# Second tower's attention: score tiles per key head, value products on 128 rows, sums from a product with ones

## The chip, the cores and the metric

The kernel runs on one core of a Trainium2 chip. The metric is device time in microseconds (us) of one execution, the median of several. The engines of the core work side by side and meet only through semaphores: TensorE (PE: matmuls, and PEld: the loads of their weights), VectorE (DVE), ScalarE (ACT), GpSimd (POOL) and SyncE (SP, which here issues most of the DMAs). A matmul reads its weights and its moving columns from SBUF and writes to PSUM, which has eight banks of 512 fp32 columns by 128 partitions.

## What is computed

A small vision tower of two levels over 16 images of 96x96, each 37 tokens (36 patches and a class token) of width 256, so 592 tokens in all. The first level is patch embedding, an attention with ternary weights and a mixture of eight experts. The second level, to which the change belongs, is two attention layers and a last linear layer:

```python
# per layer: H = 16 heads of width 16, KV = 4 key heads, 4 query heads share one
q, k = rope(q), rope(k)
q, k = qk_norm(q), qk_norm(k)           # divide by the root of the mean square
scores = einsum('bhqd,bhkd->bhqk', q, repeat(k)) / 4
scores = where(causal (and within 64 for the second layer), scores, -1e30)
probs = softmax(scores)
x = x + merge_heads(einsum('bhqk,bhkd->bhqd', probs, repeat(v))) @ wo
```

With 37 tokens the window of 64 in the second layer cuts nothing off, so both layers run the same attention; they differ in how keys and values are projected (layer 1 through a latent of width 64).

## The kernel before

The whole program is one block with one instruction stream for each engine, written out by hand; the order of the work on an engine is the order of its code, and all waits are explicit semaphore waits. The second tower is the function `l1(li)`, which each engine has for itself and calls for li = 0 and 1.

**Ahead of the attention.** Queries and keys are rotated, squared, averaged (a matmul with `mean16`) and normalised in ten units of 296 columns: `project`, `mean_square` on TensorE, `square` and `inverse_root` on ScalarE (an Ln from PSUM, L625, and an Exp, L628), `rotate` and `normalise` on VectorE (L1167, L1173). The result `qk` has 128 partitions, 32 for each key head, and five planes: plane u is the u-th query head of each of the four key heads, plane 4 the keys. `fold_keys` brings the keys into `km`, a zero-filled tile with, for each image and each pair g of key heads, 64 columns for each of the two heads e; each head's keys stand in its own 32 partitions only, by copies on ScalarE (L633) and VectorE (L1186). `take_values` (L1179) copies the values into `vo`: partitions 0 to 36 hold the even key head of a pair, 64 to 100 the odd one, with 16 columns of values and 16 columns of ones for each (the ones are written once by POOL at the start of the program). In VectorE's order `take_values` comes after the eleventh step of the unit loop (u == U + 1), two normalisations still around it.

**The attention** goes over four groups of four images. For TensorE a group is `scores(grp)` and then, one group behind, `values(grp - 1)`.

- Scores: for each image two calls, one for each pair of key heads. Weights are `km[:, b, g]`, 128 rows by 128 columns, moving columns the four query planes of the image, 148. The zeros in `km` keep the heads apart. One PSUM bank (0 to 3) holds one image: 296 columns, keys of the two heads of a pair in the two halves of the partitions.
- ScalarE takes the exponential of a bank (L668, 128x296) into `ex`, VectorE multiplies by the causal mask (L1204).
- Values: for each image two calls, weights `vo[:, b, g]`, 128 rows by 64 columns, moving 148 columns of `ex`. Of the 32 output rows of a key head 16 are values and 16 the sum of the exponentials, 16 times over, because the weights are ones. The results go to banks 4 to 7, a group taking two of them.
- ScalarE evicts them into `oz` (L652, two calls a group), VectorE moves the sums onto the value rows with a stream shuffle within 32 partitions (L1211, 128x592), ScalarE takes Ln and Exp(-x) of them for the inverse (L658, L660, 128x592), and VectorE multiplies `oz` by it into `ozp` (L1216, 128x592). ScalarE and VectorE run this over six steps: exponentials of group grp, eviction of grp - 1, inverse of grp - 2.

**After it** the output projection: for each of the five token tiles four calls (L1838) over the four planes of `ozp`, 128 weights by 256 columns; half of the contracted rows are the sums' rows, for which `wo` holds zeros. A tile waits only for the divisions of the groups that it covers. VectorE adds each tile to the residual (L755) and takes its statistics (L737); both stand behind the last division in its queue. TensorE meanwhile runs filler matmuls (`keep_clock`, L1331), and then the next stage's transposes start.

SP loads the weights of the second tower (`wq`, `wo` and others, L412) after the last expert's weights, at about 250 us, while POOL's indirect DMAs gather the expert rows (L1307) for which VectorE then waits (L1038).

Of the kernel before, what the change touches and what calls it, by code (L numbers as in the profile page):

```python
# [11 lines left out]
ALU = mybir.AluOpType  # L12
# [4 lines left out]
B = 16  # L17
# [86 lines left out]
def tower(nc, xT, tokW, sel, posb, const, iota, pairrows, small, wq0, u2t, wo0, rw, wexp,  # L104
          wqg, kvd, kug, vug, wog, wql, wvl, wol, wfin, out):
    ctx = ExitStack()
    with ctx:
# [39 lines left out]
        vo = sb("vo", [P, B, KV // 2, 2, R])  # L147
# [116 lines left out]
        ozp = ab("ozp", [P, KV, TP])  # L264
        ab("gap_a", [P, 2 * WX - 2 * U5 * T - KV * TP])
# [16 lines left out]
        l1w = DC * P * (2 * KV + 1) + 2 * KV * D + DC * LAT + P + 2 * KV * DH + DC * KV * DH - KV * DH + TP + TT * D + 2 * DC * D  # L282
        ab("gap_b", [P, 2 * WX - l1w])
        arena_b = ab("stage_l1b", [P, 2 * KV * 2 * 4 * N + 8 * T])
# [5 lines left out]
        oz = arena_b[:, 2 * KV * QT:2 * KV * QT + 4 * T].rearrange("p (u t) -> p u t", u=4)  # L290
        zs = arena_b[:, 2 * KV * QT + 4 * T:2 * KV * QT + 8 * T].rearrange("p (u t) -> p u t", u=4)
# [141 lines left out]
        def _(act):  # L433
# [176 lines left out]
            def l1(li):  # L610
# [34 lines left out]
                def evac_o(grp):  # L645
                    for i in range(2):
                        act.wait_ge(S("o_mm"), 8 * li + 2 * grp + i + 1)
                        src = bank(4 + 2 * (grp % 2) + i)[:, 0:QT].rearrange(
                            "p (a u n) -> p a u n", a=2, u=4)
                        b = 4 * grp + 2 * i  # L650
                        dst = oz.rearrange("p u (b n) -> p b u n", b=B)[:, b:b + 2]
# [10 lines left out]
                for grp in range(6):  # L662
                    if grp < 4:
                        for g in range(KV):
                            act.wait_ge(S("s_mm"), 16 * li + 4 * grp + g + 1)
                            if grp >= 2:
                                act.wait_ge(S("o_mm"), 8 * li + 2 * (grp - 1))
                            A(ex[grp % 2][:, g, :], bank(g)[:, 0:QT], ACT.Exp,  # L668
                              scale=0.25).then_inc(S("ex"), 1)
                    if 1 <= grp <= 4:  # L670
                        evac_o(grp - 1)
                    if grp >= 2:
                        inverse(grp - 2)
# [7 lines left out]
        def _(dve):  # L681
# [454 lines left out]
            def l1(li):  # L1136
# [38 lines left out]
                def take_values():  # L1175
                    dve.wait_ge(S("v1_mm"), li + 1)
                    for e in range(2):
                        r = slice(KS * e, KS * e + N)
                        last = V.tensor_copy(vo[r, :, :, e, 0:DH].rearrange("p b g d -> p (b g) d"),  # L1179
# [8 lines left out]
                for u in range(U + 3):  # L1188
# [7 lines left out]
                    if u == U + 1:  # L1196
# [10 lines left out]
                def sums(grp):  # L1207

                    dve.wait_ge(S("o"), 8 * li + 2 * grp + 2)
                    s = (slice(None), slice(None), slice(grp * 4 * N, (grp + 1) * 4 * N))  # L1210
                    V.stream_shuffle(zs[s], oz[s], [DH + i % DH for i in range(32)]).then_inc(S("zs"), 1)  # L1211

                def divide(grp):
                    s = (slice(None), slice(None), slice(grp * 4 * N, (grp + 1) * 4 * N))
                    dve.wait_ge(S("zi"), 4 * li + grp + 1)
# [794 lines left out]
```

## Time and profile before

| | us |
|---|---|
| median of three runs | 385.9 |
| all three | 385.74, 387.66, 385.9 |
| the profiled execution | 390.73 |
| span of its instructions | 388.9 |
| TensorE busy | 355.0 (91%) |
| VectorE busy | 234.6 (60%) |
| ScalarE busy | 182.3 (47%) |
| POOL busy | 132.0 (34%) |
| mean granted clock of TensorE | 0.939 |

Busy shares are averages over stages with different limits; TensorE's also counts filler matmuls. The second tower begins at about 277 us: layer 1 lasts to about 323 us, layer 2 to about 372, the last linear layer to the end. Each fp32 matmul of the program shows in the trace as two records with a weight load each. The granted clock is 1.00 at 2.4 GHz and 0.50 at 1.2 GHz.

### The profile page before, as it was taken

How to read it: one execution, taken by the hardware profiler on the slowest of the kernel's cores; microseconds unless marked ns; L12 is line 12 of the kernel's file. 1: busy time of each engine (PE TensorE's matmuls, PEld its weight loads, DVE VectorE, ACT ScalarE, POOL GpSimd, SP SyncE). 2: the span in 40 equal slices, each digit the busy share in tenths (PEclk: the TensorE clock that was granted, in tenths of full speed). 3: DMA queues.
4: the chain of work that ended last, by engine and by line, in shares of the span. 5: the costliest groups of instructions: out<-in, count | busy, mean ns of one | idle time of the engine just before them, and what ended most of it. 6: DMA issues, size and time to landing. Idle time of an engine off the chain costs nothing.

```text
span 388.9 us, 7444 instructions
## 1 busy us (share of the span) xinstructions
PE 355.0 (91%) x3038; PEld 298.5 (77%) x3038; DVE 234.6 (60%) x587; ACT 182.3 (47%) x381; POOL 132.0 (34%) x67
## 2 busy tenths in 40 slices
PE   4898989998799797999999999959899998999996
PEld 3673668876499797999899999956467985789854
DVE  1278793796666742556645555456546876548844
ACT  2010772357233143666676676311178841768500
POOL 0601029202506703787577778544200001000010
PEclk9999995798769988999999999987999999999988
DMA  8980004200222412476566571480000000000001
GB/s 282 405 300 0 3 2 148 87 3 3 81 67 73 118 71 81 121 244 200 183 202 202 186 248 43 118 312 3 1 2 2 0 3 0 0 4 0 2 0 62
DMA packets 16012, 37.55 MB, mean 97 GB/s; under 512 B 1930, under 2 KB 9729, under 8 KB 15976
## 3 DMA queue, kind: packets, MB, share of 16 engines
q1 hardware_dynamic: 14432, 33.93, 25.8%
q0 software_dynamic: 960, 2.43, 1.9%
q10 hardware_dynamic: 584, 0.69, 0.6%
q8 instruction: 25, 0.41, 0.4%
q14 instruction: 11, 0.09, 0.1%
HBM read 31.29 MB, written 5.75 MB: 95 GB/s over the span
## 4 chain that ended last, share of the span: by engine, by line
PE 55%; issue 14%; DVE 14%; ACT 8%; DMA 5%; POOL 2%; SPq 1%; POOLq 0%; ACTq 0%; DVEq 0%
PE ps L1536 9%; PE ps L1537 8%; PE ps L1538 8%; PE ps L1437 2%; PE ps L1838 2%; PE ps L1736 2%; DMA stage_l<-in_tokW 2%; PE ps L1338 2%; PE ps L1331 2%; DMA yrowhi<-yg_d,of_hi 2%; PE ps L1462 2%; PE ps L1805 2%; PE ps L1858 2%; DVE ps L1049 2%; PE ps L1449 2%
## 5 line engine op out<-in xcount | busy, mean ns | idle before, releaser
L1259 POOL TENSOR_TENSOR w1l<-raw,w1h 128x1536 fp32r<-128x1536 f32 (+1 forms) x12 | 39.8, 3318 | 35.5 <-ACT w1h L533 33.6
L1049 DVE TENSOR_TENSOR ps<-gact,ps 128x256 f32<-128x256 f32 (+3 forms) x60 | 26.3, 438 | 40.3 <-ACT gact L557 39.4
L1259 POOL TENSOR_TENSOR w0l<-raw,w0h 128x1536 fp32r<-128x1536 f32 (+1 forms) x12 | 39.9, 3322 | 29.4 <-ACT w0h L533 29.4
L1269 POOL TENSOR_TENSOR rstd<-vtmp,cst 128x5 f32<-128x5 f32 x4 | 4.7, 1172 | 112.9 <-DVE vtmp L768 64.4
L557 ACT ACTIVATE gact<-ps 128x256 f32<-128x256 f32 (+3 forms) x60 | 23.3, 388 | 25.4 <-PE ps L1538 24.8
L561 ACT ACTIVATE hrh<-ps 128x256 fp32r<-128x256 f32 (+1 forms) x48 | 18.4, 384 | 33.8 <-DVE ps L1049 33.8
L1054 DVE TENSOR_TENSOR hrl<-ps,hrh 128x256 fp32r<-128x256 f32 (+1 forms) x48 | 20.3, 423 | 18.5 <-ACT hrh L561 18.5
L1331 PE MATMUL ps<-cst 128*128 128x512 f32 x66 | 30.3, 605 | 0.0
L1536 PE MATMUL ps<-xg0h,w1h 128*128 128x256 f32 x88 | 26.4, 301 | 0.0
L1536 PE MATMUL ps<-xg1h,w0h 128*128 128x256 f32 x88 | 25.6, 291 | 0.0
L1537 PE MATMUL ps<-xg0l,w1h 128*128 128x256 f32 x88 | 25.6, 291 | 0.0
L1538 PE MATMUL ps<-xg0h,w1l 128*128 128x256 f32 x88 | 25.5, 290 | 0.0
L1537 PE MATMUL ps<-xg1l,w0h 128*128 128x256 f32 x88 | 24.9, 283 | 0.0
L1538 PE MATMUL ps<-xg1h,w0l 128*128 128x256 f32 x88 | 24.9, 283 | 0.0
L1338 PE MATMUL ps<-stage_l 128*128 128x256 f32 x60 | 17.5, 455 | 6.7 <-DMA stage_l<-in_tokW 6.7
L1331 PEld LDWEIGHTS ps<-cst 128*128 128x128 f32 x66 | 12.1, 190 | 13.0 <-issue 12.8
L1338 PEld LDWEIGHTS ps<-stage_l 128*128 128x128 f32 x60 | 13.6, 232 | 9.8 <-issue 5.1
L1805 PE MATMUL ps<-stage_l1a,km 128*128 128x148 f32 x128 | 18.0, 292 | 0.7 <-DVE vo L1179 0.7
L1805 PEld LDWEIGHTS ps<-stage_l1a,km 128*128 128x128 f32 x128 | 16.6, 188 | 2.2 <-DVE vo L1179 1.2
L1536 PE MATMUL ps<-w0h,hrh 128*128 128x256 f32 (+1 forms) x48 | 14.4, 300 | 4.1 <-DVE hrl L1054 4.1
L1536 PE MATMUL ps<-xTh,w0h 128*128 128x296 f32 x44 | 14.9, 339 | 3.4 <-DVE hsl L1054 3.4
L533 ACT ACTIVATE w0h<-raw 128x768 fp32r<-128x768 f32 (+1 forms) x24 | 18.0, 801 | 0.0
(295 smaller groups left out, 1003.1 us busy)
## 6 DMA issues: line engine op xcount, KB each, us to landing
raw<-in_wexp SPq DMA_DIRECT2D x18, 768.0 KB, 4.2
raw<-in_wexp SPq DMA_DIRECT2D x9, 640.0 KB, 4.3
xg_d<-zero SPq DMA_DIRECT2D x8, 256.0 KB, 7.7
xgs<-xg_d SPq DMA_DIRECT2D x8, 256.0 KB, 4.5
stage_l<-in_xT SPq DMA_DIRECT2D x6, 320.0 KB, 6.0
yg_d<-y SPq DMA_DIRECT2D x7, 256.0 KB, 3.3
stage_l<-in_tokW SPq DMA_DIRECT2D x6, 128.0 KB, 7.7
wq_l<-in_wql SPq DMA_DIRECT2D x1, 640.0 KB, 6.2
```

Of the source, the lines that this page charges most:

```text
L533: A(wset[x % 2][0][:, o:o + n], raw[:, o:o + n], ACT.Copy).then_inc(S("w_hi"), 1)
L557: A(gact[i % 2][rows_of(c), 0:n], gate[:, 0:n], ACT.Silu).then_inc(S("silu"), 1)
L561: A(dst[rows_of(c)], product, ACT.Copy).then_inc(S("hh"), 1)
L1049: V.tensor_tensor(up, gact[i % 2][rows_of(c), 0:n], up, ALU.mult).then_inc(S("hm"), 1)
L1054: V.tensor_tensor(dst[r], product, hi[r].bitcast(F32), ALU.subtract).then_inc(S("hl"), 1)
L1259: nc.gpsimd.tensor_tensor(wset[x % 2][1][w], raw[w], wset[x % 2][0][w].bitcast(F32), ALU.subtract).then_inc(S("w_lo"), 1)
L1331: M(bank(b), ones, cst[:, 0:BK], start=True, stop=True)
L1338: M(bank(t)[:, 0:D], xT_s[:, c, t * P:(t + 1) * P], tokW_s[:, c, :], start=(c == 0), stop=False)
L1536: M(dst, a[0], b[0], start=start, stop=False, skip_group_check=skip)
L1537: M(dst, a[0], b[1], start=False, stop=False, skip_group_check=skip)
L1538: return M(dst, a[1], b[0], start=False, stop=stop, skip_group_check=skip)
L1805: last = M(bank(i)[:, g * 4 * N:(g + 1) * 4 * N], km[:, b, g].rearrange("p e k -> p (e k)"), qk[:, 0:KV, b * N:(b + 1) * N], start=True, s ...
```

## The change

Only the second tower's attention is touched.

- **Scores** run per key head: weights `km[r, b, g, e, :]`, the 32 partitions of that head by 64 columns, moving the same 148 columns of those 32 partitions, the output in the half e of the partitions. A bank now holds two images of one pair of key heads in place of one image of two pairs; ScalarE's and VectorE's calls on it keep their shape. Semaphore counts are per half group.
- **Values and sums** are separate products. `vo` holds 16 columns for each of two key heads, so 32 columns of weights; `zo` is a fixed tile of ones and zeros of the same shape. For each image, each of the two weights, each pair of key heads and each half of the query planes there is one call of 128 rows, 32 columns of weights and 74 moving columns, its output in one quarter of the partitions: eight calls in place of two. Values land in bank 4 or 6, sums in bank 5 or 7, in the same layout, 296 columns for a group.
- **No eviction and no shuffle**: ScalarE takes Ln straight from the bank of sums into `zi` (128x296), then Exp(-x), and VectorE multiplies the bank of values by it (128x296). Values of group grp now wait for the division of grp - 2, which frees the bank.
- **Output projection**: `ozp` has two planes in place of four, without rows of sums, and the weights two blocks: two calls a tile.
- The steps of ScalarE and VectorE go over four groups in place of six; `take_values` comes one step of the loop earlier; POOL clears half of `vo` and writes `zo`; the two `wo` weights are half as large.

The core of the diff (tile shapes, `l1w`'s size and closing lines left out):

```diff
-        vo = sb("vo", [P, B, KV // 2, 2, R])
+        vo = sb("vo", [P, B, KV // 2, 2, DH])
+        zo = sb("zo", [P, 2, DH])
...
-        ozp = ab("ozp", [P, KV, TP])
+        ozp = ab("ozp", [P, 2, TP])
...
-                wo=ab(f"wo_{n}", [P, KV, D]),
+                wo=ab(f"wo_{n}", [P, 2, D]),
...
# ScalarE
-                def evac_o(grp):
-                    for i in range(2):
-                        act.wait_ge(S("o_mm"), 8 * li + 2 * grp + i + 1)
...
-                        A(dst, src, ACT.Copy).then_inc(S("o"), 1)
                 def inverse(grp):
-                    s = zs[:, :, grp * 4 * N:(grp + 1) * 4 * N]
-                    act.wait_ge(S("zs"), 4 * li + grp + 1)
-                    A(s, s, ACT.Ln).then_inc(S("lnz"), 1)
+                    z = zi[grp % 2]
+                    act.wait_ge(S("o_mm"), 4 * li + grp + 1)
+                    if grp >= 2:
+                        act.wait_ge(S("on"), 4 * li + grp - 1)
+                    A(z, bank(5 + 2 * (grp % 2))[:, 0:8 * N], ACT.Ln).then_inc(S("lnz"), 1)
                     act.wait_ge(S("lnz"), 4 * li + grp + 1)
-                    A(s, s, ACT.Exp, scale=-1.0).then_inc(S("zi"), 1)
+                    A(z, z, ACT.Exp, scale=-1.0).then_inc(S("zi"), 1)
+                for grp in range(4):
+                    for g in range(KV):
+                        act.wait_ge(S("s_mm"), 16 * li + 4 * grp + g + 1)
+                        if grp >= 2:
+                            act.wait_ge(S("o_mm"), 4 * li + grp - 1)
+                        A(ex[grp % 2][:, g, :], bank(g)[:, 0:QT], ACT.Exp,
+                          scale=0.25).then_inc(S("ex"), 1)
+                    if grp >= 1:
+                        inverse(grp - 1)
+                inverse(3)
# VectorE
-                    if u == U + 1:
+                    if u == U:
                         take_values()
...
-                def sums(grp):
-                    dve.wait_ge(S("o"), 8 * li + 2 * grp + 2)
...
-                    V.stream_shuffle(zs[s], oz[s], [DH + i % DH for i in range(32)]).then_inc(S("zs"), 1)
                 def divide(grp):
                     dve.wait_ge(S("zi"), 4 * li + grp + 1)
-                    V.tensor_tensor(ozp[s], oz[s], zs[s], ALU.mult).then_inc(S("on"), 1)
+                    V.tensor_tensor(ozp[:, :, grp * 4 * N:(grp + 1) * 4 * N],
+                                    bank(4 + 2 * (grp % 2))[:, 0:8 * N].rearrange("p (u c) -> p u c", u=2),
+                                    zi[grp % 2].rearrange("p (u c) -> p u c", u=2), ALU.mult).then_inc(S("on"), 1)
+                mask(0)
+                for grp in range(4):
+                    if grp + 1 < 4:
+                        mask(grp + 1)
+                    divide(grp)
# TensorE, scores
+                    for half in range(2):
+                        if grp >= 1:
+                            pe.wait_ge(S("ex"), 16 * li + 4 * (grp - 1) + 2 * half + 2)
+                        if grp == 0 and half == 1:
+                            pe.wait_ge(S("vo"), li + 1)
+                        for i in range(2):
+                            b = 4 * grp + 2 * half + i
+                            for kv in range(KV):
+                                g, e = divmod(kv, 2)
+                                r = slice(R * kv, R * kv + R)
+                                ins = M(bank(2 * half + g)[KS * e:KS * e + KS, i * 4 * N:(i + 1) * 4 * N],
+                                        km[r, b, g, e, :], qk[r, 0:KV, b * N:(b + 1) * N],
+                                        start=True, stop=True, skip_group_check=True)
+                                if i == 1 and e == 1:
+                                    ins.then_inc(S("s_mm"), 1)
# TensorE, values
+                    if grp >= 2:
+                        pe.wait_ge(S("on"), 4 * li + grp - 1)
                     for i in range(4):
                         b = 4 * grp + i
+                        if i % 2 == 0:
+                            pe.wait_ge(S("exm"), 16 * li + 4 * grp + i + 2)
+                        for x, w in enumerate((vo[:, b], None)):
+                            dst = bank(4 + 2 * (grp % 2) + x)[:, 0:8 * N].rearrange("p (u c) -> p u c", u=2)
+                            for g in range(KV // 2):
+                                lhs = (zo[:, :, :] if w is None else w[:, g]).rearrange("p e d -> p (e d)")
+                                for uh in range(2):
+                                    r = R * (2 * g + uh)
+                                    o = i % 2 * 4 * N + uh * 2 * N
+                                    last = M(dst[r:r + R, :, i * N:(i + 1) * N], lhs,
+                                             ex[grp % 2][:, i // 2 * 2 + g, o:o + 2 * N].rearrange("p (u n) -> p u n", u=2),
+                                             start=True, stop=True, skip_group_check=True)
+                    last.then_inc(S("o_mm"), 1)
# TensorE, projection
-                    for g in range(KV):
+                    for k in range(2):
-                        last = M(bank(t)[:, 0:D], ozp[:, g, t * P:(t + 1) * P],
-                                 w["wo"][:, g, :], start=(g == 0), stop=(g == KV - 1))
+                        last = M(bank(t)[:, 0:D], ozp[:, k, t * P:(t + 1) * P],
+                                 w["wo"][:, k, :], start=(k == 0), stop=(k == 1))
```

## Rows read from the trace of the kernel before

**Rows 1.** Chain of waits, 280 to 323 us: start, duration, what, records.

```profile
283.97 1.00 PE ps L1736 x4
...
300.39 2.79 PE ps L1805 x20
...
304.33 2.21 PE ps L1805 x16
306.54 1.16 PE ps L1822 x16
...
312.32 8.85 PE ps L1838 x40
...
321.65 0.44 DVE stats L737
```

**Rows 2.** Groups by line, 280 to 389 us: shapes, count, busy us, mean ns.

```profile
L652 ACT ACTIVATE stage_l1b<-ps 128x296 f32<-128x296 f32 x16 | 6.5, 419 | 1.5 <-PE ps L1822 1.0
L1216 DVE TENSOR_TENSOR ozp<-stage_l1b 128x592 f32<-128x592 f32 x8 | 6.2, 775 | 3.5 <-ACT stage_l1b L660 3.5
...
L658 ACT ACTIVATE stage_l1b<-stage_l1b 128x592 f32<-128x592 f32 x8 | 5.5, 687 | 0.0
```

**Rows 3.** Timeline of layer 2 and the last stage: start, duration, engine, what.

```profile
361.36 8.90 PE L1838 MATMUL ps<-wo_l,ozp 128*128 128x256 f32 x40
...
378.22 6.03 PE L1858 MATMUL ps<-wfs,xnT 128*128 128x256 f32 x16
```

**Rows 4.** Timeline of VectorE after the last division of layer 1.

```profile
316.93 0.42 DVE L755 TENSOR_TENSOR xres<-xres,ps 128x256 f32<-128x256 f32 x1
...
317.73 0.40 DVE L755 TENSOR_TENSOR xres<-xres,ps 128x256 f32<-128x256 f32 x1
```

**Rows 5.** Timeline of TensorE, small tiles elsewhere: weights rows*columns, moving.

```profile
39.66 0.46 PE L1379 MATMUL ps<-stage_l,cst 128*32 128x148 f32 x8
40.24 2.25 PE L1387 MATMUL ps<-stage_l,sq 128*32 128x148 bf16 x128
...
78.50 1.34 PE L1437 MATMUL ps<-stage_l 32*37 32x37 f32 x64
...
341.97 3.95 PE L1770 MATMUL ps<-wvl_s,xnT 128*64 128x32 f32 x128
```

**Rows 6.** Groups by line, 280 to 389 us: the 296-column operations.

```profile
L625 ACT ACTIVATE stage_l1a<-ps,cst 128x296 f32<-128x296 f32 x20 | 9.9, 494 | 3.7 <-PE ps L1746 3.7
...
L1167 DVE TENSOR_TENSOR stage_l1a<-ps,cst 128x296 f32<-128x296 f32 x20 | 9.3, 467 | 12.3 <-PE ps L1736 11.7 <-PE ps L1733 0.6
...
L628 ACT ACTIVATE stage_l1a<-stage_l1a 128x296 f32<-128x296 f32 x20 | 9.0, 450 | 0.6
```

**Rows 7.** Timeline at the start of layer 1's attention.

```profile
298.95 1.38 DVE L1179 COPY vo<-ps 37x512 f32<-37x512 f32 x2
...
300.18 3.44 ACT L668 ACTIVATE stage_l1b<-ps 128x296 f32<-128x296 f32 x8
...
301.86 3.11 DVE L1204 TENSOR_TENSOR stage_l1b<-stage_l1b,cst 128x296 f32<-128x296 f32 x8
```

**Rows 8.** DMA issues (KB, us to landing); the chain, 240 to 276 us.

```profile
wo_g<-in_wog SPq DMA_DIRECT2D x1, 512.0 KB, 5.2
...
252.05 7.36 DMA yrowhi<-yg_d,of_hi
```

**Rows 9.** Stretches: length; busy and records by engine; granted clock, DMA share, GB/s.

```profile
60.00:65.00 5.00, 5.00 (x96) 4.08 (x95) 2.13 (x6) 0.20 (x1) 4.92 (x4) 0.50 0.48 161
75.00:80.00 5.00, 5.00 (x176) 4.39 (x176) 4.66 (x16) 3.19 (x6) 0.00 (x0) 1.00 0.02 5
...
250.00:260.00 10.00, 7.29 (x60) 6.99 (x58) 4.92 (x12) 2.67 (x7) 4.71 (x5) 1.00 0.97 339
261.00:265.00 4.00, 2.92 (x12) 2.63 (x13) 2.51 (x6) 1.58 (x2) 1.62 (x1) 0.50 0.04 13
...
342.00:346.00 4.00, 4.00 (x130) 3.96 (x130) 0.98 (x3) 1.81 (x5) 0.00 (x0) 1.00 0.01 4
```

More of the change, by code:

```diff
@@ L289, in tower @@
               for i in range(2)]
-        oz = arena_b[:, 2 * KV * QT:2 * KV * QT + 4 * T].rearrange("p (u t) -> p u t", u=4)
-        zs = arena_b[:, 2 * KV * QT + 4 * T:2 * KV * QT + 8 * T].rearrange("p (u t) -> p u t", u=4)
+        zi = [arena_b[:, 2 * KV * QT + i * 8 * N:2 * KV * QT + (i + 1) * 8 * N] for i in range(2)]
         stage1.close()
@@ L1178, in take_values @@
                         r = slice(KS * e, KS * e + N)
-                        last = V.tensor_copy(vo[r, :, :, e, 0:DH].rearrange("p b g d -> p (b g) d"),
+                        last = V.tensor_copy(vo[r, :, :, e, :].rearrange("p b g d -> p (b g) d"),
                                              bank(3)[r, :].rearrange("p (c d) -> p c d", d=DH))
@@ L1797, in scores @@
                         pe.wait_ge(S("kfd"), 4 * (li + 1))
-                    for i in range(4):
-                        b = 4 * grp + i
+                    for half in range(2):
                         if grp >= 1:
-                            pe.wait_ge(S("ex"), 16 * li + 4 * (grp - 1) + i + 1)
-                        if grp == 0 and i == 3:
+                            pe.wait_ge(S("ex"), 16 * li + 4 * (grp - 1) + 2 * half + 2)
+                        if grp == 0 and half == 1:
                             pe.wait_ge(S("vo"), li + 1)
-                        for g in range(KV // 2):
-                            last = M(bank(i)[:, g * 4 * N:(g + 1) * 4 * N],
-                                     km[:, b, g].rearrange("p e k -> p (e k)"),
-                                     qk[:, 0:KV, b * N:(b + 1) * N],
-                                     start=True, stop=True, skip_group_check=True)
-                        last.then_inc(S("s_mm"), 1)
+                        for i in range(2):
[8 more added lines that the diff above has]
+                                    ins.then_inc(S("s_mm"), 1)
                 def values(grp):
@@ L1821, in values @@
-                        for g in range(KV // 2):
-                            last = M(dst[2 * R * g:2 * R * (g + 1)],
-                                     vo[:, b, g].rearrange("p e r -> p (e r)"),
-                                     ex[grp % 2][:, i, g * 4 * N:(g + 1) * 4 * N],
-                                     start=True, stop=True, skip_group_check=True)
-                        if i % 2 == 1:
-                            last.then_inc(S("o_mm"), 1)
+                        if i % 2 == 0:
+                            pe.wait_ge(S("exm"), 16 * li + 4 * grp + i + 2)
@@ L1829, in l1, with project_out @@
+                    last.then_inc(S("o_mm"), 1)
+                def project_out(t):
+                    pe.wait_ge(S("on"), 4 * li + (min((t + 1) * P, T) - 1) // (4 * N) + 1)
+                    for k in range(2):
+                        last = M(bank(t)[:, 0:D], ozp[:, k, t * P:(t + 1) * P],
+                                 w["wo"][:, k, :], start=(k == 0), stop=(k == 1))
+                    last.then_inc(S("wo1_mm"), 1)
                 for grp in range(5):
@@ L1834, in l1 @@
                 for t in range(TT):
-                    pe.wait_ge(S("on"), 4 * li + (min((t + 1) * P, T) - 1) // (4 * N) + 1)
-                    for g in range(KV):
-                        last = M(bank(t)[:, 0:D], ozp[:, g, t * P:(t + 1) * P],
-                                 w["wo"][:, g, :], start=(g == 0), stop=(g == KV - 1))
-                    last.then_inc(S("wo1_mm"), 1)
+                    project_out(t)
             l1(0)
```

44 lines of the change are left out of this document (8 added, 36 removed).

## The prediction

> **What bounds the kernel now.** I read the chain of waits first, then the groups by line, then the timeline of one attention stage. The span is 388.9 us and the profiled execution's own time 390.73 us, so 1.8 us lie around the span; the median of the three timed runs is 385.9 us, 4.8 us less. All sums are made against 390.73 and carried over to the median.
>
> In the chain [rows 1] the reader is to see that from 300.39 to 321.17 us TensorE alone carries the time: scores of 16 records in 2.21 us, values of 16 records in 1.16 us, over and over, and then the output projection, 40 records in 8.85 us without a stop. (Every fp32 matmul call shows as two records: the 20 calls of the projection are 40.) One group of four images costs 2.21 + 1.16 = 3.37 us of TensorE. ScalarE is close behind: four exponentials at 3.44/8 = 0.43 [rows 7], two evictions at 0.42, a Ln and an Exp over 592 columns at 0.69 each [rows 2] are 3.94 us a group. The second layer repeats the first to 0.01 us (projection of 8.90 us from 361.36, [rows 3]), so a gain counts twice.
>
> **The output projection.** 40 records become 20 per layer, same shape, 8.85/40 = 0.221 us each: 4.43 us. It has bounded the end alone, so 4.42 us per layer go from TensorE. What is late next is VectorE: the additions and statistics of the five tiles stand behind the last division in its queue and cost 0.80 us a tile back to back (316.93 to 317.73, [rows 4]).
>
> **Scores.** A group goes from 8 calls (16 records, 128 rows of weights) to 16 calls (32 records, 32x64 weights) with the same 148 columns. Consecutive calls use another 32 rows and the other half of the columns. Nearest rows: values now run 128x64, alternating halves, 148 columns, at 1.16/16 = 0.072 us a record, against 0.138 for the full array [rows 1]; so two halves of the columns overlap. Whether different rows overlap too, no row shows. If not, 32 x 0.072 = 2.3 us a group, about today's 2.21. If so, half of it, 0.036. The floor is the fastest 64-wide row: 128 records in 3.95 us, 0.031 each [rows 5], 1.0 us a group. I take 0.038, 1.2 us, since each call names its own rows and its own bank or half bank, so nothing is shared; 2.3 stays as the bad end.
> The Trainium skill ("TensorE: Matmul & The Clock Gate", part 3) says that matmuls on different 32-row groups run side by side, four of them measured at 3.07 times one; by it the group is near 1.2 us. No row of this trace shows it.
>
> **Values and sums.** Two calls of 148 columns per image become eight of 74 with 32 columns of weights: 64 records a group. A 74-column record streams for a quarter of a 296-column one, whose four take 1.00 us [rows 1], so 0.062 us. Four column quarters overlap: a bf16 matmul with 32 columns of weights, whose 148 columns take one pass and thus also 0.062 us, runs 128 records in 2.25 us, 0.018 each, and fp32 with 32 columns of weights does 8 records of 148 columns in 0.46 us [rows 5]. The fp32 32x37 tiles take 1.34/64 = 0.021. So 0.018 to 0.021, 1.2 us a group, equal to today's 1.16; the bad end is 0.031 (the 64-wide row), 2.0 us.
> The same page of the Trainium skill has two rules against this change: the sequencer's microcode needs about 62 ns per matmul, which would make 64 records 4.0 us, and starts never come closer than about 25 ns, which would make them 1.6 us (TensorE then 2.8 us a group). The trace has 18 and 21 ns between records [rows 5], so by it neither holds here.
>
> **ScalarE.** Per layer eight evictions of 0.42 go. Ln and Exp now run on 296 columns, Ln straight from PSUM: the same two operations on 296 columns are 0.494 and 0.450 [rows 6]. A group is 4 x 0.43 + 0.95 = 2.7 us. With TensorE at 1.2 + 1.2 = 2.4, ScalarE becomes the bound of the steady part, 2.7 for 3.37. **VectorE**: the shuffle goes, the division falls from 0.775 [rows 2] to about 0.47 (a 296-column product from PSUM, [rows 6]), masks stay at 3.11/8 = 0.39 [rows 7]: about 2.0 us, hidden under ScalarE. Values of group g now wait for the division of group g-2, which reads PSUM; behind that wait stand the next scores, and by the walk below it has ended 0.8 us before, so it costs nothing; a division later than that would stop TensorE for the rest.
>
> **Start of the stage.** The copy of values moves up one normalisation: its input is long there, because the copy starts at 298.95 only [rows 7], behind a normalisation that waits for ScalarE. It now runs in that wait and is over before today's 300.33, so that the last scores, which start behind it at 300.39 [rows 1], no longer wait. The first mask (301.86) comes up to 0.9 us earlier, 1.38 of copies less 0.47 for the normalisation; in layer 2 the values are there only at 345.9 [rows 5], still in time. But ScalarE's first exponential stays at 300.18, behind its own key copies.
>
> **Walk through layer 1**, each step from the prices above. Exponentials of groups 0 and 1: 300.18 to 303.65. Second scores wait for the first two exponentials (301.1), end 302.5; values 0 end 303.8, visible at 304.0. Inverse 0 to 305.0, exponentials 2 to 306.7, inverse 1 to 307.65, exponentials 3 to 309.4, inverse 2 to 310.35. The last mask ends 309.85, the last values 310.5, visible 310.75; inverse 3 to 311.7, last division 312.2. The projection begins at 310.5 and never waits for a division (its fourth tile starts at 313.15): it ends 314.93. Residual tiles on VectorE go from 312.2, the fifth at 315.4, statistics end 316.25. Today they end 322.09 (321.65 + 0.44, [rows 1]). Gain 5.8 us a layer, 11.7 in both.
>
> **Loads.** Each layer's projection weights shrink from 512 to 256 KB. They are issued at 251 and 252 us, while the gather on the chain waits 7.36 us for its data, with all 16 DMA engines at 0.97 [rows 8, 9]. Half a megabyte less at the 339 GB/s of that stretch is 1.5 us; the first gathered tile is not the last in the queues, so between 0 and 1.5, I take 1.0. The clears of the small tiles by POOL halve at the very start; their readers come in the second tower, so nothing.
>
> Sum: 390.73 - 11.7 - 1.0 = 378.0 in the profiled execution's terms, 385.9 - 12.7 = **373.2 us** for the median.
>
> **Clock.** The granted clock is 1.00 (2.4 GHz) all through both attention stages, even for the 64-wide, 32-column records at 342 to 346, but 0.50 (1.2 GHz) in 60:65 among 32-row tiles, in 261:265 after TensorE idled for some 4 us behind the gather [rows 9]. The fillers between layers stay, while VectorE's end now trails the projection by 1.3 us instead of 0.9, so 0.4 us more idle. The last stage's 16 projection records take 6.03 us, a pace of the low level [rows 3], 0.377 each against 0.221: up to 2.5 us either way if the fall comes elsewhere. A shorter gather wait could also keep the clock in 261:265, where TensorE works 2.92 us at half speed: up to 1.5 us less.
>
> **Rivals.**
> A: one packing fails. Scores at 2.3 us: the walk gives TensorE 3.5 us a group but an earlier start, last values 313.2, projection 317.6, statistics 318.7: gain 3.4 a layer, 385.9 - 6.8 - 1 = 378. Values at 2.0 instead: last values 312.9, statistics 318.6, the same 378. For it: no row with different rows side by side. Against: the 18 ns rows. Both fail: TensorE needs 4.3 us a group, last values 316, statistics 321.5: 384.
> B, slower than before: TensorE falls to 1.2 GHz in the attention stages because records are shorter and ScalarE makes it wait. For it: 60:65 ran such tiles at 0.50. Against: 75:80, the same mix, at 1.00. Scores 2.4, values 2.2: last values at 301.1 + 3 x 2.4 + 4 x 2.2 = 317.1, projection 20 x 0.43 = 8.6 to 325.7, statistics 326.8: 4.7 more a layer, 385.9 + 9.4 - 1 = 394. It decides once three groups of scores, four of values and the projection need over 19.7 us together (12.8 in the forecast). In one layer alone: about 384.
> C: the edit does its part but a phase of the low clock takes some back in the last stage: 375 to 376.
>
> **From numbers to chances.** A measurement of this kernel can tell 0.5% (1.9 us) from no change. Forecast with its clock play, 370.5 to 375: 0.57. C: 0.08. A with one failing: 0.22. Both failing or one layer at 1.2 GHz (384): 0.07, on the edge of no change. B: 0.06. The range 370 to 381 leaves out about 2 in 10. Faster 0.89, same 0.05, slower 0.06.
>
> **What would show it.** Right: score records spaced 0.03 to 0.04 us, value records 0.018 to 0.021, the projection of 20 records in 4.4 us, exponentials without gaps behind the inverse, and the last statistics of a layer some 16 us after its first exponential (21.9 today). Wrong: ScalarE waiting for scores (A), a granted clock under 1.00 between 298 and 366 (B), the projection waiting for the last division, or the gather still landing after 7.4 us.

## The result, and the profile after

| | before | after |
|---|---|---|
| median of four runs, us | 386.78 | 372.45 |
| lowest and highest | 385.74 to 390.29 | 369.74 to 374.77 |
| the profiled execution | 390.73 | 373.38 |
| span of its instructions | 388.9 | 371.6 |
| mean granted clock | 0.939 | 0.940 |

After to before is 0.961, with an interval of 0.952 to 0.971: 14.3 us less by the medians. Ratios and intervals, here and below, leave out executions over 1.5% above the fastest of their kernel and the medians do not, so a ratio is not the quotient of its two medians. The forecast was 373.2 us, its range 370 to 381.

The page of the changed kernel, busy time by engine:

```profile
PE 337.0 (91%) x3510; PEld 281.1 (76%) x3510; DVE 221.5 (60%) x571; ACT 171.0 (46%) x365; POOL 130.7 (35%) x68
```

TensorE lost 18 us of busy time and kept its share of 91%. Fillers count in both, so the share does not say what sets the pace; the chain does.

The chain of waits of the changed kernel through layer 1's attention (start, duration, what, records), which answers to [rows 1]:

```profile
298.70 0.73 ACT stage_l1b L660 x2
...
299.48 1.35 PE ps L1792 x32
300.83 1.17 PE ps L1816 x64
302.00 1.17 PE ps L1792 x32
303.16 1.16 PE ps L1816 x64
304.33 1.17 PE ps L1792 x32
305.49 1.21 PE ps L1816 x64
306.72 0.43 ACT stage_l1b L651
...
313.08 0.44 DVE stats L728
...
313.54 0.46 DVE mv L734 x5
```

The reader is to see two things. Scores fell from 2.21 to 1.17 us a group while values, with four times the records, stayed at 1.16; and the two follow each other on TensorE without a gap, 2.33 us a group for 3.37. The projection has left the chain: from 306.72 on the chain goes through the inverse, the division and VectorE's additions, beside which the 20 records run:

```profile
305.20 1.32 ACT L660 ACTIVATE stage_l1b<-ps 128x296 f32<-128x296 f32 x4
...
308.00 4.58 PE L1825 MATMUL ps<-wo_g,ozp 128*128 128x256 f32 x20
```

(Timeline of layer 1: start, duration, engine, line, count, in brackets the idle time before.) From the first exponential to the aggregation of the statistics that is 313.54 - 298.70 = 14.84 us, where it was 21.93 by the same two marks. Layer 2 takes the same 14.84. Twice 7.09 is 14.2 us, and the medians differ by 14.3. The profiled executions differ by 17.35; the 3.1 us beyond come in with a start of the stage that is 1.5 us earlier and a last stage that is 1.65 us shorter, and both vary from run to run (below).

The same stage in the groups by line of the changed kernel (280 to 372 us: count, busy us, mean ns, idle before), beside [rows 2] and [rows 6]:

```profile
L660 ACT ACTIVATE stage_l1b<-ps 128x296 f32<-128x296 f32 x32 | 10.7, 416 | 0.4 <-PE ps L1792 0.4
...
L651 ACT ACTIVATE stage_l1b<-ps 128x296 f32<-128x296 f32 x8 | 3.3, 418 | 2.8 <-PE ps L1816 1.7 <-DVE ozp L1200 1.0
```

An exponential has a mean of 0.416 us, yet 32 of them keep ScalarE busy for 10.7 us only, 0.33 each: back to back they overlap. That is the number the prediction had wrong. In the steady part ScalarE now waits for TensorE once a group, 0.20 us ahead of its Ln:

```profile
304.39 0.42 ACT L651 ACTIVATE stage_l1b<-ps 128x296 f32<-128x296 f32 x1 [0.20 <-PE ps L1816]
```

The windows of both attentions and of the last stage (length, busy and records by engine, granted clock, DMA share, GB/s), beside [rows 9]:

```profile
296.00:309.00 13.00, 11.68 (x394) 9.41 (x393) 10.36 (x25) 11.11 (x30) 0.00 (x0) 1.00 0.01 4
340.00:354.00 14.00, 12.68 (x378) 10.64 (x371) 11.72 (x30) 9.30 (x26) 0.00 (x0) 1.00 0.02 4
362.00:364.00 2.00, 2.00 (x5) 1.62 (x6) 0.11 (x1) 0.00 (x0) 0.00 (x0) 0.50 0.00 0
```

The clock stays at 2.4 GHz through both attentions; it is at 1.2 GHz in part of the last stage, as before.

### The profile page after: what moved, and what is told of

It reads as the page before. It is cut to its first block, busy times and chain, and to the rows that moved or that the text cites. A ratio compares the mean times of both kernels' runs of the same rounds, so it can differ in the third digit from the quotient of the medians.

```text
span 371.6 us, 8361 instructions
## 1 busy us (share of the span) xinstructions
PE 337.0 (91%) x3510; PEld 281.1 (76%) x3510; DVE 221.5 (60%) x571; ACT 171.0 (46%) x365; POOL 130.7 (35%) x68
## 3 DMA queue, kind: packets, MB, share of 16 engines
HBM read 30.76 MB, written 5.75 MB: 98 GB/s over the span
## 4 chain that ended last, share of the span: by engine, by line
PE 50%; DVE 17%; issue 15%; ACT 13%; DMA 2%; POOL 2%; SPq 1%; POOLq 0%; ACTq 0%; DVEq 0%
PE ps L1520 8%; PE ps L1522 7%; PE ps L1521 7%; DVE ps L1040 3%; ACT w1h L533 3%; PE ps L1421 3%; ACT w0h L533 2%; DMA stage_l<-in_tokW 2%; PE ps L1720 2%; PE ps L1315 2%; PE ps L1446 2%; PE ps L1433 2%; PE ps L1322 2%; PE ps L1853 2%; ACT gact L557 1%
## 5 line engine op out<-in xcount | busy, mean ns | idle before, releaser
L1322 PE MATMUL ps<-stage_l 128*128 128x256 f32 x60 | 16.1, 427 | 6.9 <-DMA stage_l<-in_tokW 6.9
L1322 PEld LDWEIGHTS ps<-stage_l 128*128 128x128 f32 x60 | 12.5, 213 | 9.6 <-issue 4.8
L1520 PEld LDWEIGHTS ps<-xg0h,w1h 128*128 128x128 f32 x88 | 17.6, 200 | 0.6 <-issue 0.2
L533 ACT ACTIVATE w1h<-raw 128x768 fp32r<-128x768 f32 (+1 forms) x24 | 17.8, 800 | 0.0
L1521 PEld LDWEIGHTS ps<-xg0l,w1h 128*128 128x128 f32 x88 | 17.7, 201 | 0.0
L1522 PEld LDWEIGHTS ps<-xg0h,w1l 128*128 128x128 f32 x88 | 17.7, 201 | 0.0
```

Source lines behind the costliest of these rows:

```text
L533: A(wset[x % 2][0][:, o:o + n], raw[:, o:o + n], ACT.Copy).then_inc(S("w_hi"), 1)
L1322: M(bank(t)[:, 0:D], xT_s[:, c, t * P:(t + 1) * P], tokW_s[:, c, :], start=(c == 0), stop=False)
L1520: M(dst, a[0], b[0], start=start, stop=False, skip_group_check=skip)
L1521: M(dst, a[0], b[1], start=False, stop=False, skip_group_check=skip)
L1522: return M(dst, a[1], b[0], start=False, stop=stop, skip_group_check=skip)
```

## The experiments

All but the last were timed against the kernel before on the same chip. A layer's price is read between the two `rstd` operations of POOL that close layers 1 and 2 (timelines of POOL before and after):

```profile
323.24 1.17 POOL L1269 TENSOR_TENSOR rstd<-vtmp,cst 128x5 f32<-128x5 f32 x1 [48.47 <-DVE vtmp L778]
371.95 1.17 POOL L1269 TENSOR_TENSOR rstd<-vtmp,cst 128x5 f32<-128x5 f32 x1 [47.53 <-DVE vtmp L768]
```

```profile
314.68 1.17 POOL L1253 TENSOR_TENSOR rstd<-vtmp,cst 128x5 f32<-128x5 f32 x1 [41.38 <-DVE vtmp L769]
356.30 1.17 POOL L1253 TENSOR_TENSOR rstd<-vtmp,cst 128x5 f32<-128x5 f32 x1 [40.45 <-DVE vtmp L759]
```

They are 48.71 us apart before and 41.62 after, and 41.62 again in a second profile of the changed kernel, whose total differed by 1.5 us. The granted clock between the two marks was 1.00 in every profile, but for the run with the tiles alone. So this price repeats far better than the total.

**The score tiles alone**, in the kernel before.

```diff
-                        for g in range(KV // 2):
-                            last = M(bank(i)[:, g * 4 * N:(g + 1) * 4 * N],
-                                     km[:, b, g].rearrange("p e k -> p (e k)"),
-                                     qk[:, 0:KV, b * N:(b + 1) * N],
+                            for kv in range(KV):
+                                g, e = divmod(kv, 2)
+                                r = slice(R * kv, R * kv + R)
+                                ins = M(bank(2 * half + g)[KS * e:KS * e + KS, i * 4 * N:(i + 1) * 4 * N],
+                                        km[r, b, g, e, :], qk[r, 0:KV, b * N:(b + 1) * N],
```

> The kernel before with only the packed scores (per key head, 32 rows by 64 columns of weights). Attention stage of a layer, first exponential to last statistics, was 21.9 us before and is 14.8 after. Theory: scores fall from 2.21 to 1.17 us a group, but ScalarE (four exponentials 1.32, two evictions 0.93, Ln and Exp 1.41: 3.7 us a group) becomes the bound, so the stage gets at most 2 us shorter (about 20), the kernel about 3 to 4 us faster. Rival: TensorE alone sets the pace, then the whole 2.8 us a layer of the steady part comes (stage 19.1, kernel 5.6 us faster) and the removal of evictions and shuffle was worth nothing.

Measured: 383.24 us against 385.99, ratio 0.989 (0.981 to 0.997); the layer 47.83, 0.88 less. The chain of this kernel:

```profile
306.86 0.78 DVE ozp L1216
307.64 0.77 DVE stage_l1b L1204 x2
...
308.54 1.39 PE ps L1826 x16
```

TensorE saves 4 x 0.97 = 3.9 us of scores a layer, and three quarters of it turn into waiting: the last values start at 308.54 because their masks stand in VectorE's queue behind a division that waits for ScalarE's inverse. So the faster scores are worth little without the removal of the evictions, the shuffle and half of the inverse. The expected bound of 2 us for the stage held; the total stays within 2% of the kernel before.

**Scores on the full array**, in the changed kernel.

```diff
-                            for kv in range(KV):
-                                ...
-                                ins = M(bank(2 * half + g)[KS * e:KS * e + KS, i * 4 * N:(i + 1) * 4 * N],
-                                        km[r, b, g, e, :], qk[r, 0:KV, b * N:(b + 1) * N],
+                            for g in range(KV // 2):
+                                ins = M(bank(2 * half + g)[:, i * 4 * N:(i + 1) * 4 * N],
+                                        km[:, b, g].rearrange("p e k -> p (e k)"),
+                                        qk[:, 0:KV, b * N:(b + 1) * N],
```

> The changed kernel with the scores undone: 128 rows by 128 columns of weights, two calls an image, same banks. Theory: TensorE bounds the steady part, 2.33 us a group, so 3 groups of scores at 1.04 us more each are +3.1 us a layer, stage 17.9, kernel +6 us against the changed one. Rival (the prediction's own walk, ScalarE at 2.7 us a group is the bound and hides a part): +2.0 us a layer, kernel +4.

Measured: 375.62 against 385.99, 0.966 (0.956 to 0.976); the layer 44.26, 2.64 more than after.

```profile
298.71 2.28 PE ps L1790 x16
...
302.16 2.21 PE ps L1790 x16
...
305.54 2.21 PE ps L1790 x16
307.75 2.23 PE ps L1815 x128
```

Three groups of scores stand on this chain, 6.70 us where they were 3.69, and nothing but TensorE is between them. Of the 3.0 us the two last groups of values give 0.3 back: 2.23 us together, against 1.21 and the 1.30 to the projection at 308.00, for their masks are now ready ahead of them. The same edit is thus worth 0.9 us a layer in the old kernel and 2.6 in the new one. That lies between the 3.1 of the expectation and the 2.0 of its rival, nearer to the first; the median, 3.2 us above the 372.45 of another chip, could not have told them apart.

**The projection twice.**

```diff
-                    for k in range(2):
+                    for k in (0, 1, 0, 1):
```

> The changed kernel with every call of the output projection issued twice (40 records a layer, result unchanged). Theory: the projection is on the path call by call, 20 records of 0.221 are +4.4 us, less what VectorE's tail of 0.8 us a tile trails now: stage 19.0, kernel +8.5 us. Rival: VectorE bounds the tail after the change, TensorE has slack there, then under +3 us a layer.

Measured: 377.57 against 385.99, 0.977 (0.968 to 0.985); the layer 45.94, 4.32 more.

```profile
301.99 8.84 PE ps L1825 x40
```

The projection is back on the chain, at the length of [rows 1]. The halved projection gives 4.3 of the 7.1 us of a layer. (The three parts that were put back, this one, the scores and the copy of values below, cost 4.32, 2.64 and 0.76 us, together more than the 7.1: they are not independent. The evictions, the shuffle and the longer inverse were not put back by themselves.)

**Neighbours on the same rows**: the same 32 score records, but each pair of calls uses the same rows and the same half of the columns.

```diff
-                        for i in range(2):
-                            b = 4 * grp + 2 * half + i
-                            for kv in range(KV):
-                                g, e = divmod(kv, 2)
+                        for kv in range(KV):
+                            g, e = divmod(kv, 2)
+                            for i in range(2):
+                                b = 4 * grp + 2 * half + i
```

> The changed kernel with the same score calls in another order: the two images of one key head follow each other, so that neighbours share rows, columns and bank, in place of four neighbours on four different row groups. Theory: what makes a score record cost 0.036 us is that neighbours run side by side on different rows; with equal neighbours pairs serialise, 0.07 us a record or more, group of scores 2.3 us, stage +3.3 us or more, kernel +6.6. Rival: the pace is that of issue or of the small weight load (about 0.03 us a record) whatever the neighbour, then nothing changes (stage 14.8).

Measured: 372.25 against 385.99, 0.961 (0.954 to 0.969); the layer 41.71, 0.09 more.

```profile
302.98 1.23 PE ps L1792 x32
```

1.23 for 1.17: the order in which the tiles alternate hardly matters here. The theory of the expectation, 3.3 us a layer, failed, and its rival, a pace set by issue or by the small weight load, fits; only the tiles alone (below) decide between them. The starts of single records in this trace show how the order loses its effect: in the first group of scores they come in fours, 12 to 19 ns apart within the four. The record that signals its completion as the eighth of its sixteen in the program is the fourteenth to start, behind records of other tiles that the program has after it. So records of different tiles do not start in the order of the program; what arranges them the trace does not show.

**The copy of values one step later**, as it was.

```diff
-                    if u == U:
+                    if u == U + 1:
                         take_values()
```

> The changed kernel with take_values back at its old place, one normalisation later. Theory: the second half of the first scores and the first masks start about 1 us later, and as TensorE is the bound from the first values on, 0.5 to 1.0 us a layer comes back (stage 15.3 to 15.8, kernel +1 to +2). Rival (the prediction: ScalarE's first exponential does not move, so the end does not): stage 14.8, no change.

Measured: 371.31 against 384.66, 0.961 (0.950 to 0.973); the layer 42.38, 0.76 more. (One of the four executions took 627.34 us, the others 368.94 to 372.84; no trace shows why.)

```profile
292.06 0.70 DVE vo L1170
...
292.81 0.74 PE ps L1792 x16
```

The second half of the first scores waits for the copy, as at 300.39 in [rows 1], and the third exponential for those scores. VectorE, which has its key copies still to do behind it, starts the masks 1.69 us after the first exponential (294.29, 292.60), against 0.76 in the changed kernel. The total does not show it, the layer does, within the 0.5 to 1.0 us that were expected: 0.76 us twice is less than the scatter of the total.

**Weights of 512 KB again**, the second half unused.

```diff
-                wo=ab(f"wo_{n}", [P, 2, D]),
+                wo=ab(f"wo_{n}", [P, 4, D]),
```

> The changed kernel with projection weights loaded at their old size, 512 KB a layer in place of 256 (the second half is not used). Theory of the prediction: the gather of the last experts' rows lands up to 1.5 us later, 1.0 taken. Rival: the gather's packets are served in turn with the loads, so the size of what stands beside it does not matter, 0 to 0.3 us. The profile's wait of VectorE for the gather (first landing 7.36 us after the issue before) decides rather than the whole time, which scatters by more.

Measured: 370.78 against 384.66, 0.958 (0.949 to 0.967); the layer 41.61. The gather, from its first issue to VectorE's first use, took 259.61 - 252.83 = 6.78 us here, and in the changed kernel:

```profile
251.26 0.96 POOL L1291 DMA_INDIRECT yrowhi<-yg_d,of_hi  x1 [2.78 <-DMA yg_d<-y]
...
258.03 0.48 DVE L1029 SCALAR_TENSOR_TENSOR h<-yrowhi,whi,h 128x256 f32<-128x256 f32 x1 [1.93 <-DMA yrowhi<-yg_d,of_hi]
```

6.77 us. Over all profiles, the eleven with small loads took 6.39 to 7.13, 6.66 in the mean, and the three with large ones 7.46 (before), 7.16 (the score tiles alone) and 6.78 (here). The means differ by 0.5 us, but the one kernel in which nothing but the size was changed lies within the range of the small loads, so a saving of that size can't be told from none. The 1.0 us of the prediction is not borne out.

**The product of sums twice.**

```diff
-                        for x, w in enumerate((vo[:, b], None)):
+                        for x, w in ((0, vo[:, b]), (1, None), (1, None)):
```

> The changed kernel with every product with ones issued twice (96 records of values and sums a group, result unchanged). Theory: TensorE bounds the steady part at 2.33 us a group and a record of this shape costs 0.018, so +0.58 us in each of four groups, +2.3 us a layer, stage 17.1, kernel +4.6 us. Rival (ScalarE bounds with 2.7 us a group, as predicted): TensorE has 0.3 us to spare a group, at most +1.2 us a layer.

Measured: 376.29 against 384.66, 0.974 (0.964 to 0.984); the first stage 17.3 us, 2.46 more, the layer 44.67, 3.05 more.

```profile
299.22 1.68 PE ps L1816 x96
300.90 1.17 PE ps L1792 x32
302.07 1.81 PE ps L1816 x96
```

32 records more cost 0.51 and 0.65 us on the chain in the first two groups, and 1.4 us together in the last two, of which 0.41 is a pause (below). At 0.018 us each the 128 records of a layer are 2.3 us: each microsecond added to TensorE lengthens the stage by about one, so TensorE and not ScalarE bounds the steady part. (The rival allowed at most 1.2 us.) Layer 2 paid 0.6 us more than layer 1. TensorE pauses in both layers without a wait that the profile shows, 0.41 us in layer 1 and 0.72 in layer 2:

```profile
352.26 0.26 PE L1816 MATMUL ps<-stage_l1b,vo 128*32 128x74 f32 x3 [0.72 <-issue]
```

The longer pause is half of the 0.6; what the engine did in the pauses stays open.

**The last key copies later**: behind ScalarE's first exponentials and VectorE's first masks, since only the third group of scores needs them.

```diff
# ScalarE, VectorE: ahead of the attention
-                take_keys(1)
# ScalarE, behind the exponentials of the group
+                    if grp == 0:
+                        take_keys(1)
# VectorE
                 mask(0)
+                take_keys(1)
```

> The changed kernel with the copies of the second half of the keys moved behind the first group's exponentials (ScalarE) and masks (VectorE); they are needed only by the third group's scores. Theory: the first exponential waits only for ScalarE's key copies (0.84 us), so the whole attention stage starts about 0.75 us earlier in each layer and nothing else is late: kernel -1.5 us. Rival: the copies now delay the second exponentials and masks by the same amount, no gain.

Measured: 367.57 against 384.66, 0.950 (0.942 to 0.959); the layer 40.89, 0.73 less than after.

```profile
298.31 0.62 ACT stage_l1b L659 x2
...
298.98 1.35 PE ps L1793 x32
...
301.49 0.10 issue
301.58 1.24 PE ps L1793 x32
```

The exponentials start at once behind the last normalisation's part on ScalarE (297.87 + 0.45). The scores at 301.58, those of the third group, now start 0.10 us late, where the copies delayed the whole stage before: 0.73 us gained of the 0.75 expected.

**Again, and one step further.** The changed kernel and the one with later key copies ran once more on one chip, with a third that also puts the last layer's bias products ahead of its transposes, among the fillers.

```diff
-            keep_clock(3, 7)
-            transposes(4)
-
+            keep_clock(2, 7)
             pe.wait_ge(S("var"), NORMS)
-            for t in range(4):
+            for t in range(3):
                 bias(t)
+            keep_clock(1, 3)
+            transposes(4)
+            keep_clock(1, 3)
+            bias(3)
```

> The changed kernel once more beside e8 and e9: 372 us, attention stage 14.8 us in each layer.

> The kernel of e8 once more, on the chip on which e9 and the changed kernel run: 1.5 us faster than the changed kernel, from 0.73 us in each layer, by the theory; by the rival of e9 the scatter of the low clock's phase hides it.

> The kernel of e8 with one more step: the bias products of the last stage (1.7 to 2.2 us of TensorE behind the last transposes, where they end 1.2 us after the transposed activations are ready) go ahead of the transposes into the time in which TensorE ran fillers for lack of work; one filler stands between. Theory: the last projection starts 0.8 to 1.2 us earlier, kernel 1 us faster than e8 (366.5). Rival: the granted clock falls earlier or longer, as the busy stretch ahead of the last projection is another one, and takes it back or more (368 to 369).

Measured, against 385.17: the changed kernel 369.85, 0.960 (0.955 to 0.964), its stage again 14.84; later key copies 369.02, 0.961 (0.955 to 0.967), the layer 40.89 again; with the bias products 366.62, 0.957 (0.949 to 0.964). The intervals overlap. What the totals disagree on lies outside the two layers, ahead of them and behind. Ahead: the gather of `yrowhi` is first issued at 251.26 us in the changed kernel and at 248.34 in the same kernel again, at 251.85 and 246.87 in the two profiles with later key copies, and the granted clock from 60 to 100 us differs with it (changed kernel, and the same again):

```profile
60.00:100.00 40.00, 36.48 (x684) 29.79 (x680) 29.41 (x92) 17.43 (x28) 14.15 (x7) 0.82 0.22 73
```

```profile
60.00:100.00 40.00, 34.53 (x633) 27.16 (x632) 33.57 (x98) 19.94 (x31) 16.68 (x8) 0.94 0.25 78
```

Behind: the clock in the last stage. Its 16 projection records, first in the changed kernel, the same kernel again and the last one:

```profile
361.78 5.13 PE L1853 MATMUL ps<-wfs,xnT 128*128 128x256 f32 x16
```

```profile
358.81 6.60 PE L1853 MATMUL ps<-wfs,xnT 128*128 128x256 f32 x16
```

```profile
355.95 3.72 PE L1857 MATMUL ps<-wfs,xnT 128*128 128x256 f32 x16
```

The same code took 5.13 and 6.60, and 3.72 where the granted clock was 1.00 throughout. So the 1.65 us that the last stage seems to gain in the first pair of profiles is scatter: in the second profile of the changed kernel it is as long as before. The bias products' new place is worth 13.68 - 13.44 = 0.24 us of last stage against the first profile with later key copies, in which the 16 records took 3.72 too. They start 5.09 us behind the last `rstd` instead of 5.25, so 0.16 us earlier where 0.8 to 1.2 was expected: that theory missed, and the 366.62 so near to its 366.5 is luck. Whether the new place makes the full clock likelier three timed rounds do not settle; without it the records took 3.72 once and 5.41 once. By the median this is the best version run, by the ratio the first run with later key copies (0.950) is, and the 0.73 us a layer of the key copies is the part that is shown.

**Tiles alone**: in layer 2, after its fillers, six runs of 64 records with nothing to wait for, apart by a filler (none between e and f): (a) one tile of 32 rows by 64 columns of weights, (b) four such tiles in turn, (c) one row group, both column halves, (d) one column half, two row groups, (e) 128 rows by one quarter of the columns, (f) four quarters in turn.

```diff
+                    for j in range(32):    # b; the others alike
+                        r = slice(32 * (j % 4), 32 * (j % 4) + 32)
+                        M(bank(5 + j % 4 // 2)[64 * (j % 2):64 * (j % 2) + 64, 0:148], cst[r, 0:64], cst[r, 0:148],
+                          start=True, stop=True, skip_group_check=True)
```

> Not for the time of the kernel: in the second layer, after the fillers, five runs of small fp32 matmuls stand by themselves, 64 records each, 148 columns on 32 rows by 64 columns of weights unless said otherwise. a: all on one tile. b: the four tiles of the scores in turn. c: same rows, the two column halves in turn. d: same column half, two groups of rows in turn. e: 74 columns on 128 rows by 32 columns of weights, all on one quarter of the columns; f: the four quarters in turn. Theory 1 (tiles run side by side, each record streams for 0.123 us, or 0.062 with 74 columns, and a queue behind each tile hides a bad order, which is why e4 changed nothing): a 0.12 us a record or more, c and d half, b a quarter (0.036); e 0.06 or more, f 0.018. Theory 2 (a small tile's record is cheap by itself, bound by issue or weight load): all of a to d 0.036, e and f 0.018.

One execution, 411.87 us. The timeline of TensorE, a to f, and windows, two in a and one each in b, d and e:

```profile
315.22 13.34 PE L1702 MATMUL ps<-cst 32*64 32x148 f32 x64
330.49 2.81 PE L1706 MATMUL ps<-cst 32*64 32x148 f32 x64
334.29 4.24 PE L1710 MATMUL ps<-cst 32*64 32x148 f32 x64
340.43 8.16 PE L1715 MATMUL ps<-cst 32*64 32x148 f32 x64
350.52 5.02 PE L1719 MATMUL ps<-cst 128*32 128x74 f32 x63
...
355.40 1.22 PE L1721 MATMUL ps<-cst 128*32 128x74 f32 x61
```

```profile
315.20:318.00 2.80, 2.80 (x23) 2.79 (x23) 1.35 (x5) 0.00 (x0) 0.00 (x0) 1.00 0.00 0
318.00:320.00 2.00, 2.00 (x11) 1.83 (x10) 0.00 (x0) 0.00 (x0) 0.00 (x0) 0.52 0.00 0
...
332.00:334.00 2.00, 2.00 (x46) 1.33 (x38) 0.00 (x0) 0.00 (x0) 0.00 (x0) 1.00 0.04 8
...
342.00:344.00 2.00, 2.00 (x20) 1.88 (x18) 0.00 (x0) 0.00 (x0) 0.00 (x0) 0.50 0.03 8
...
352.00:354.00 2.00, 2.00 (x32) 2.00 (x31) 0.00 (x0) 0.00 (x0) 0.00 (x0) 0.95 0.00 0
```

On one tile a record takes about 0.125 us at 2.4 GHz (some 22 in the first 2.8 us) and 0.25 at 1.2 GHz (the other 42 in 10.5). Two row groups with the same columns take 8.16/64 = 0.127 at 1.2 GHz, half of it: different rows do run side by side. Two column halves take 0.066. Four tiles take 0.044, the first of them at the low clock. One column quarter takes about 0.064 where the clock is back (352:354), and four quarters in turn 0.020. So the first theory holds and the second, cheap records whatever the neighbour, is excluded: that is what the prediction found in no row.

## Why the prediction was right, step by step

- **Scores.** 1.2 us a group forecast, 1.17 measured, 0.037 a record. Rival A (rows in turn do not overlap) is excluded by the tiles alone, and the full-array run shows what it would have cost, 2.6 us a layer. With that the trace agrees with the rule of the Trainium skill ("TensorE: Matmul & The Clock Gate", part 3) that row groups run side by side.
- **Values and sums.** 1.2 forecast, 1.16 measured, 0.018 a record. The same page of the Trainium skill gives a floor of about 25 ns between starts, which does not hold in this trace either. It gives the 62 ns of microcode per matmul only for hardware decode switched off, a condition that the prediction left out; at 18 ns a record nothing like it shows.
- **Projection.** 4.43 us for the 20 records forecast, 4.58 measured from the first one's start to the last one's end; 4.3 us a layer by the doubling. VectorE is late next, as said: from the projection's start to the last statistics' end 5.52 us, 5.75 forecast.
- **ScalarE as the bound: wrong.** The prediction took 3.44/8 = 0.43 for an exponential [rows 7]. In those rows ScalarE was waiting for scores between the calls: the first three start 0.30 to 0.32 us apart, the last five 0.50. So the row holds the pace of the scores and not the engine's. Without waits four take 1.32 us, 0.33 each (the timeline above), and a group costs ScalarE 1.32 + 0.42 + 0.45 = 2.2 us, not 2.7. TensorE, 2.33, remains the bound, which the doubled sums confirm. From the first exponential to the projection the walk had 10.3 us and the chip took 9.3: 0.3 of it before the first values' end, 0.7 in the groups behind. This is the mis-sized term. With 0.2 us less from the projection's start to the last statistics it makes the difference: a stage gains 7.1 us, not 5.8, so 2.5 us in both layers.
- **Start of the stage.** The first exponential stays behind ScalarE's key copies, as said. The copy of values no longer holds up the last scores of the first group, and the masks come 0.9 us earlier, as said too; the prediction gave that no price of its own (its walk only had no wait there), and putting the copy back shows 0.76 us a layer.
- **Loads.** 1.0 us forecast, none shown; the means of large and small loads differ by 0.5 us, within their scatter.
- **The sum.** The stages give 14.2 us where 11.7 was forecast, the loads nothing shown where 1.0 was: 14.2 against 12.7, and the medians say 14.3. The forecast of 373.2 lies 0.7 us above the measured 372.45, closer than its terms were, because the median before was 386.78 in these runs, 0.9 above the 385.9 from which it set out, and the two errors in the terms went opposite ways: that closeness is luck.
- **Clock.** 1.00 in both attentions, so rival B did not occur. Of the 2.5 us either way in the last stage the downward side is real: against 6.03 us the same 16 records took 3.72 to 6.78 over all profiles. The clock ahead of the second tower moves the total as much (the first issue of the `yrowhi` gather lies between 245.38 and 252.83 us over all profiles), and the prediction had no term for it.

## What to carry to other kernels

Before a mean or a row's pace is taken for an engine's price, look whether the engine waited inside the row: the busy total over the count, in a stretch without waits, is the price (0.33 us here, not 0.43 or 0.416). Work on a small contraction can be cut into tiles of 32 rows and work with few output columns into quarters, at about a quarter of the time per record (0.037 us for 0.138 with the scores), so that zeros and duplicate sums need not be computed. Price such an edit together with what stands behind it: the score tiles were worth 0.9 us a layer while ScalarE and VectorE were late, and 2.6 once their work was gone.

## What the runs showed of the hardware

- The granted clock fell from 1.00 to 0.50 while TensorE was busy without a pause, 2.00 of 2.00 us, on a single tile of 32 rows by 64 columns, and it was at 0.50 again in the run on two row groups (342:344). It came back to 1.00 in the run on four tiles (332:334) and in the one on 128 rows by a quarter of the columns (352:354, 0.95). In the attention, with all rows in use, it stayed at 1.00. A busy engine alone did not keep it.
- Score records in pairs on the same tile cost 1.23 us a group against 1.17 in turn, though the same tile alone takes 0.125 us a record. In the trace of the pairs, records of other tiles that stand behind one in the program start ahead of it (the eighth of sixteen starts as the fourteenth).
- Four tiles of 32 rows by 64 columns, which between them touch every row, but of each row only half of the columns, take 0.037 us a record, 0.125/3.4; four column quarters take 0.018 to 0.020.
